# The next graph's input norm, moved from VectorE to ScalarE in two blocks of four tiles, in an attention loop with hand-written queues

## Chip, cores, metric

One core of one Trainium2 chip runs one program. The metric is the device time of one launch in microseconds (us). The kernel before takes 1538.24 us, the median of three runs (1538.18 to 1538.66).

## What is computed

Two layers over eight graphs of 1024 nodes with 128 features, all in fp32. The change lies in the second layer's graph attention, of which this is the reference, cut to what matters:

```
x = x + _L1_gnn_ref(_layernorm(x), adj, W_lin, b_lin, W_q, W_k, ln_g, ln_b)

X = heads(leaky_relu(xn @ W_lin + b_lin))           # 4 heads of 32 columns
q = heads(leaky_relu(xn @ W_q)); k = heads(leaky_relu(xn @ W_k))
att = sigmoid(einsum('bhxd,bhyd->bhxy', q, k) * scale)
adj_h = adj[:, None] * att
deg = sum(adj_h, -1); dis = where(deg > 0, deg ** -0.5, 0)
Y = (dis[..., :, None] * adj_h * dis[..., None, :]) @ X
out = layernorm(Y) * ln_g + ln_b
```

Here xn is `_layernorm(x)`, that is (x - mean) / sqrt(var + 1e-5) over the 128 features. Making xn of the next graph is the step that the change touches. Layer 1 (a graph convolution and a mixture of experts) and the layer after the attention (slices and a state-space mixer) are untouched.

## The kernel before

The program is a row of stages; `attention_gnn_stage` is the third and takes from about 668 to 1200 us of the profile. Each engine has a queue written out by hand: a double loop over i (B + 2 turns, i = 0 to 9) and n (16 steps), with semaphores between the engines. Nothing reorders a queue, so an instruction that waits holds up all behind it.

In turn i, step n stands for one of 2 x 8 pairs (half of the 1024 columns, tile of 128 rows) of graph i. Around it:

- TensorE: `products(i', n')` of 18 steps ago into YA, `scores(i, n)` into S (it waits for the sigmoid of the step before, since S has one buffer), `degrees` of two steps ago into DG (it waits for VectorE's multiply of that step), and a side job into the one buffer M. The list SIDE gives the side jobs by step: at 6 and 7 `x0` and `x1` (the product with W_lin), at 8 and 9 `xn0` and `xn1` (transposes of the next graph's normalised input X, which wait for `xn_ready`), at 3 and 5 `y0` and `y1`, at 2 and 10 the degrees, and the q and k products.
- ScalarE: the sigmoid of S into AH (128x2048, sets `att_ready`), and between sigmoids the copies out of PSUM.
- VectorE: `multiply(g)`, AH times the adjacency tile, 128x2048; between multiplies the small work: `stats_x(i + 1)` (statistics of the next graph's input, at step 4 for i = 0 and 1 and at step 0 for later i, by STATS_AT), `scale_X(i - 1, 1)` at step 4, `scale_Y` at 3 and 5, `stats_y` behind multiply(5), `make_X` ahead of multiply(6) and multiply(7), and so on. `apply_x(i + 1)` stands at step 6 for i = 0 and 1 and at step 4 for i = 2 to 6, behind multiply and, at step 4, behind `scale_X`. `apply_next`, for what follows the last graph, stands in turn 7.
- GpSimd: the power -0.5 of variances (`rstd_ready`) and of degrees, gathers of rows for graph i + 2 by indirect DMA, their sums (L1251, L1254), and the addition of a shift to R (L1287).
- SyncE: the loads of adjacency tiles and of X, and `keep_x`, which stores X before it is normalised in place (`x_kept`).

In the trace the input X bears the name `x`, YT the name `carry`. The norm's statistics and `apply` are in the class LayerNorm, lines 124 to 142: `apply` is eight VectorE instructions (x - mean) * rstd of 128x128 each, L142. Other lines of use: L1417 sigmoid, L1447 multiply, L1314 scores, L1327 products, L1341 degrees, L1370 the side product of x0 and x1, L1500 the tile product of scale_X, L1508 scale_Y, L1543 make_X. The front stage normalises on ScalarE with the same form as the change, at L777.

Of the kernel before, what the change touches and what calls it, by code (L numbers as in the profile page):

```python
# [7 lines left out]
ALU = mybir.AluOpType  # L8
ACT = mybir.ActivationFunctionType
AX = mybir.AxisListType  # L10

P = 128
B, N, D = 8, 1024, 128
T = N // P
# [16 lines left out]
STATS_AT = (4, 4)  # L31
# [11 lines left out]
class Chain:  # L43
# [13 lines left out]
    def wait(self):  # L57

        self.eng.wait_ge(self.sem, self.base + self.n)
# [1014 lines left out]
def is_graph(i):  # L1074
    return 0 <= i < B


def stats_step(i):

    return STATS_AT[i] if i < len(STATS_AT) else 0  # L1080
# [27 lines left out]
def attention_gnn_stage(nc, x_in, ys, slots, kept, X, W, Gt, xnT, Wc, YT, dis_last, x_out, adjT, b_lin, ln_g, ln_b, W_x, b_xT, W_sliceT, b_slice,  # L1108
# [6 lines left out]
    with ExitStack() as ctx:  # L1115
        sb = lambda name, shape, dt=fp32: ctx.enter_context(nc.sbuf_tensor("c_" + name, shape, dt))
        ps = lambda name, shape: ctx.enter_context(nc.psum_tensor("c_" + name, shape, fp32))
        sem = lambda name: ctx.enter_context(nc.semaphore("c_" + name))

        bias, gain, shift = sb("bias", [P, D]), sb("gain", [P, D]), sb("shift", [P, D])  # L1120
# [10 lines left out]
        DS = sb("DS", [P, HALF])  # L1131
        deg, mask, raw = sb("deg", [P, T, HEADS]), sb("mask", [P, T, HEADS]), sb("raw", [P, T, HEADS])
        dis = [sb("dis0", [P, T, HEADS]), dis_last]

        S = ps("S", [P, HEADS, HALF])
        YA = ps("YA", [P, NH, HALF])
# [6 lines left out]
        norm_in = LayerNorm(lambda n, s: sb("i" + n, s), lambda n: sem("i" + n))  # L1143
        norm_y = LayerNorm(lambda n, s: sb("y" + n, s), lambda n: sem("y" + n))
        pair_ready, x_ready, x_kept = sem("pair_ready"), sem("x_ready"), sem("x_kept")
        xn_ready = sem("xn_ready")
        side_full, side_free = sem("side_full"), sem("side_free")
        s_psum, att_ready = sem("s_psum"), sem("att_ready")
        ah_dve = sem("ah_dve")
# [238 lines left out]
        @block.scalar  # L1388
        def _(act):
            def copy_xnT(i, half):  # L1390
                act.wait_ge(side_full, full[f"xn{half}", i])
                act.activation(xnT[:, cols(half)], M[:, :], ACT.Copy).then_inc(side_free, 1)

            def copy_qk(dst, i, name):
                act.wait_ge(side_full, full[name, i])
                act.activation(dst[:, cols(int(name[-1]))], M[:, :], ACT.Copy).then_inc(side_free, 1)

            def copy_Y(i, half):
                wait(act, side_full, full[f"y{half}", i - 1] if i > 0 else 0)
                act.wait_ge(y_psum, STEPS * i + T * half + T)  # L1400
                act.activation(YT[:, cols(half)], YA[:, half, :], ACT.Copy).then_inc(yT_ready, 1)

            def copy_degrees(i, half):
                act.wait_ge(dg_psum, NH * i + half + 1)
                if half:
                    act.wait_ge(side_full, full["deg0", i])
                elif i > 0:
                    act.wait_ge(side_full, full["deg1", i - 1])
                act.activation(DS[:, :], DG[:, :], ACT.Copy).then_inc(ds_ready, 1)

            for i in range(B + 2):
                for n in range(STEPS):
                    g = STEPS * i + n
                    if is_graph(i):
                        act.wait_ge(s_psum, g + 1)
                        wait(act, y_psum, g - UNITS + 1)
                        act.activation(AH[g % UNITS][:, :, :], S[:, :, :], ACT.Sigmoid, scale=HD ** -0.5).then_inc(att_ready, 1)  # L1417
                    if n == 0 and is_graph(i):
                        copy_qk(K, i, "k1")
                    if n == 1 and is_graph(i):  # L1420
                        copy_qk(Q, i, "q1")
                    if n == 1 and is_graph(i - 1):
                        copy_degrees(i - 1, 1)
                    if n == 2 and is_graph(i - 2):
                        copy_Y(i - 2, 1)
                    if n == 9 and is_graph(i):
                        copy_degrees(i, 0)
                    if n == 10 and is_graph(i - 1):
                        copy_Y(i - 1, 0)
                    if i < B and n in (8, 9):  # L1430
                        copy_xnT(i + 1, n - 8)
                    if is_graph(i + 1):
                        if n == 11:
                            copy_qk(Q, i + 1, "q0")
                        if n == 13:
                            copy_qk(K, i + 1, "k0")

        @block.vector
        def _(dve):
# [39 lines left out]
                                            norm_in.rstd[(B - 1) % 2][:, t:t + 1], ALU.subtract, ALU.mult)  # L1479
                ins.then_inc(xn_ready, 1)  # L1480

            def apply_x(i):
                dve.wait_ge(x_kept, 16 * i)
                norm_in.apply(dve, X, X, i - 1, (i - 1) % 2).then_inc(xn_ready, 1)

            def read_degrees(i, half):
                dve.wait_ge(side_full, full[f"deg{half}", i])
# [60 lines left out]
            for i in range(B + 2):  # L1548
                for n in range(STEPS):
                    if n == 2 and is_graph(i - 1):  # L1550
                        read_degrees(i - 1, 1)
                    if n == 3 and is_graph(i - 2) and i - 2 < B - 1:
                        scale_Y(i - 2, 0)
                    if n == 5 and is_graph(i - 2) and i - 2 < B - 1:
                        scale_Y(i - 2, 1)
                    if n in (6, 7) and is_graph(i):
                        make_X(i, n - 6)
                    if n == 10 and is_graph(i):
                        read_degrees(i, 0)
                    if is_graph(i):  # L1560
                        multiply(STEPS * i + n)
                    if n == stats_step(i) and i < B:
                        stats_x(i + 1)
                    if n == 1 and is_graph(i):
                        leak_qk(K, i, "k1")
                    if n == 2 and is_graph(i):
                        leak_qk(Q, i, "q1")
                    if n == 4 and is_graph(i - 1):
                        scale_X(i - 1, 1)
                    if n == (6 if i < len(STATS_AT) else 4) and is_graph(i + 1):  # L1570
                        apply_x(i + 1)
                    if n == 4 and i + 1 == B:
                        apply_next()
                    if n == 7 and i + 1 == B:
                        fold_weights()
                    if n == 12 and i + 1 == B:
                        read_fold()
                    if n == 5 and is_graph(i - 2) and i - 2 < B - 1:
                        stats_y(i - 2)
                    if n == 8 and is_graph(i - 2) and i - 2 < B - 1:  # L1580
                        gain_Y(i - 2)
                    if n == 9 and is_graph(i - 2) and i - 2 < B - 1:
                        finish(i - 2)
                    if n == 12 and is_graph(i + 1):
                        leak_qk(Q, i + 1, "q0")
                    if n == 14 and is_graph(i + 1):
                        leak_qk(K, i + 1, "k0")
                    if n == 15 and is_graph(i):
                        scale_X(i, 0)
# [913 lines left out]
```

## Time and profile before

| | |
|---|---|
| median of three runs | 1538.24 us |
| the profiled execution | 1539.02 us |
| its span in the profile | 1537.3 us |
| TensorE busy | 91% of the span |
| VectorE busy | 66% |
| ScalarE busy | 49% |
| GpSimd busy | 47% |
| mean granted TensorE clock | 0.984 of full |

All times in the rows further down are in us from the start of the span, of this one profiled execution. A row of the view in order of time gives start, duration, engine, line, operation, output and inputs with their shapes, and how many instructions are merged in the row; the brackets give the idle time before it and what ended it. PE is TensorE, PEld its weight load, DVE VectorE, ACT ScalarE, POOL GpSimd. A merged row's duration runs from its first start to its last end.

### The profile page before, as it was taken

To read this page: it belongs to the slowest core of one execution; us is meant where nothing else is said; L and a number is where in the kernel's file an instruction comes from. 1 tells how busy PE (TensorE), PEld (TensorE's weight loads), DVE (VectorE), ACT (ScalarE), POOL (GpSimd) and SP (SyncE) were. 2 spreads that over 40 slices of the span, in tenths; PEclk is the share of its full clock that TensorE was granted. 3 is DMA by queue.
4 is the path that set the end of the run, shared out by engine and by line. 5 is a ranking of instruction groups with operands and counts; after the bars stand their busy time and mean duration, and the time that the engine had idled before them with its cause. 6 is when DMAs were issued, how large, how long until landed. Compare 5 with 4: busy or idle time off the path is not lost. (4 is left out here: it accounts for less than half of the span.)

```text
span 1537.3 us, 25067 instructions
## 1 busy us (share of the span) xinstructions
PE 1401.7 (91%) x9010; PEld 808.8 (53%) x9010; DVE 1021.2 (66%) x2212; ACT 748.2 (49%) x1184; POOL 720.7 (47%) x500
## 2 busy tenths in 40 slices
PE   4999999899999999977899988998999779999998
PEld 2455545669999998732222222222222357773488
DVE  2467767633333333368788999999987789967732
ACT  3365565534444444446454554655554457872110
POOL 1127776740000000749787887876233479981000
PEclk9999999999999999999999999999999999999999
DMA  9757637276788775633342424423322231004024
GB/s 300 254 188 282 235 118 228 88 205 203 229 230 231 233 228 159 171 118 125 96 129 90 124 84 122 142 84 119 91 90 69 69 95 42 15 1 90 1 85 138
DMA packets 207599, 215.26 MB, mean 140 GB/s; under 512 B 23269, under 2 KB 164709, under 8 KB 207476
## 3 DMA queue, kind: packets, MB, share of 16 engines
q1 hardware_dynamic: 199284, 196.81, 41.9%
q0 software_dynamic: 8192, 16.86, 3.5%
q8 instruction: 72, 1.18, 0.3%
q14 instruction: 51, 0.42, 0.1%
HBM read 168.54 MB, written 45.07 MB: 139 GB/s over the span
## 5 line engine op out<-in xcount | busy, mean ns | idle before, releaser
L1417 ACT ACTIVATE c_AH<-c_S 128x2048 f32<-128x2048 f32 x128 | 240.6, 1879 | 235.5 <-PE c_S L1314 235.5
L1447 DVE TENSOR_TENSOR c_AH<-c_AH,c_A 128x2048 f32<-128x2048 f32 x128 | 313.0, 2454 | 44.2 <-ACT c_AH L1417 43.9
L1242 POOL DMA_INDIRECT G<-ys,slots x102 | 195.4, 1915 | 32.7 <-issue 28.0
L810 ACT ACTIVATE a_A<-a_DG,a_A 128x256 f32<-128x256 f32 (+1 forms) x192 | 93.8, 527 | 208.3 <-PE a_DG L677 207.0
L530 POOL DMA_INDIRECT rows<-a_S,a_slots x128 | 134.0, 1047 | 49.9 <-issue 38.1
L557 POOL DMA_INDIRECT a_A<-ys,slots x16 | 16.4, 1024 | 292.9 <-DMA ys<-a_A 288.3
L1341 PE MATMUL c_DG<-c_AH,c_ones 128*32 128x512 f32 x1024 | 138.1, 612 | 12.0 <-DVE c_AH L1447 12.0
L1327 PE MATMUL c_YA<-c_AH,c_XT 128*32 128x512 f32 x1024 | 137.9, 620 | 12.1 <-DVE c_XT L1500 12.1
L1314 PE MATMUL c_S<-c_Q,c_K 32*128 32x512 f32 x928 | 135.2, 653 | 14.5 <-DVE c_K L1532 7.8
L648 PE MATMUL a_AG<-a_A,x 128*128 128x512 f32 x256 | 114.1, 599 | 5.1 <-DVE a_Z L891 5.1
L677 PE MATMUL a_DG<-a_A 128*128 128x256 f32 (+1 forms) x336 | 99.9, 420 | 7.1 <-ACT a_A L810 6.0
L690 PE MATMUL a_AG<-a_A 128*128 128x128 f32 x848 | 102.9, 277 | 0.0
L690 PEld LDWEIGHTS a_AG<-a_A 128*128 128x128 f32 x848 | 99.8, 194 | 3.5 <-issue 3.4
L1314 PEld LDWEIGHTS c_S<-c_Q,c_K 32*128 32x128 f32 x928 | 36.9, 186 | 116.6 <-ACT c_AH L1417 52.8
L690 PE MATMUL a_TP<-a_A 128*128 128x128 f32 x800 | 96.3, 275 | 0.0
L690 PEld LDWEIGHTS a_TP<-a_A 128*128 128x128 f32 x800 | 93.2, 192 | 2.9 <-issue 2.9
L1234 POOL TENSOR_TENSOR c_raw<-c_deg,c_power 128x16 f32<-128x16 f32 x16 | 73.0, 4562 | 36.0 <-DVE c_deg L1490 35.8
L677 PE MATMUL a_FG<-a_A 128*128 128x256 f32 (+1 forms) x312 | 86.0, 398 | 0.0
L648 PEld LDWEIGHTS a_AG<-a_A,x 128*128 128x128 f32 x256 | 47.3, 190 | 69.5 <-issue 59.4
L985 DVE COPY a_A<-a_AG 128x256 f32<-128x256 f32 x71 | 30.1, 424 | 75.0 <-PE a_AG L658 75.0
L1341 PEld LDWEIGHTS c_DG<-c_AH,c_ones 128*32 128x32 f32 x1024 | 20.4, 108 | 112.2 <-issue 83.8
L1697 POOL TENSOR_TENSOR s_SW<-s_SW,s_top 128x512 f32<-128x512 f32 x64 | 67.0, 1048 | 25.7 <-DVE s_top L1883 25.3
(393 smaller groups left out, 2566.2 us busy)
## 6 DMA issues: line engine op xcount, KB each, us to landing
a_A<-in_dram SPq DMA_DIRECT2D x72, 578.0 KB, 4.0
a_A<-in_dram SPq DMA_DIRECT2D x32, 1024.0 KB, 10.0
c_A<-in_dram SPq DMA_DIRECT2D x128, 256.0 KB, 2.8
a_A<-rows SPq DMA_DIRECT2D x71, 129.0 KB, 3.3
ys<-a_A SPq DMA_DIRECT2D x71, 128.0 KB, 2.3
a_X<-in_dram SPq DMA_DIRECT2D x8, 512.0 KB, 13.0
a_R<-in_dram SPq DMA_DIRECT2D x8, 512.0 KB, 5.3
stream<-a_R SPq DMA_DIRECT2D x8, 512.0 KB, 10.0
```

The lines of the kernel that those rows point to most:

```text
L530: pool.indirect_dma_start(rows, bass.IndirectOffsetOnAxis(ap=slots[:, k, T * i + t:T * i + t + 1], axis=0), S[i % 3][k][:, t, :], None, bo ...
L648: mm = pe.matmul(AG[:, half(h)], F[:, t, :], adj(i)[:, t, half(h)], start=(t == 0), stop=(t == T - 1))
L677: pe.matmul(up_bank(g, f)[:, 0:n], w_of(g)[:, f * P:(f + 1) * P], xT_of(g)[:, 0:n], start=True, stop=True).then_inc(up_psum, 1)
L690: mm = pe.matmul(YB[g % 2][:, t, :], hT[g % 2][:, f, t * P:(t + 1) * P], w_of(g)[:, F_N + FT + f * D:F_N + FT + (f + 1) * D], start=(f == ...
L810: act.activation(hT[g % 2][:, f, 0:size(g)], up_bank(g, f)[:, 0:size(g)], ACT.Gelu, bias=w_of(g)[:, F_N + f:F_N + f + 1]).then_inc(h_ready, 1)
L1234: pool.tensor_tensor(raw[:, tiles(half), :], deg[:, tiles(half), :], power[:, :].rearrange("p (t h) -> p t h", h=HEADS)[:, tiles(half), :] ...
L1242: pool.indirect_dma_start(Gt[k][:, t, :], None, ys, bass.IndirectOffsetOnAxis(ap=slots[:, k, T * i + t:T * i + t + 1], axis=0), bounds_che ...
L1314: mm = pe.matmul(S[:, h, :], keys[rows, t * P:(t + 1) * P], queries[rows, :], start=True, stop=True)
L1327: mm = pe.matmul(YA[h * HD:(h + 1) * HD, half, :], XT[:, t, h * HD:(h + 1) * HD], ah[:, h, :], start=(t == 0), stop=(t == T - 1))
L1341: mm = pe.matmul(DG[h * HD:(h + 1) * HD, :], ones[:, :], ah[:, h, :], start=(t == 0), stop=(t == T - 1))
L1417: act.activation(AH[g % UNITS][:, :, :], S[:, :, :], ACT.Sigmoid, scale=HD ** -0.5).then_inc(att_ready, 1)
L1447: dve.tensor_tensor(ah[:, :, :], ah[:, :, :], A[g % ADJ_BUFS][:, :].unsqueeze(1).to_broadcast([P, HEADS, HALF]), ALU.mult).then_inc(ah_dve, 1)
```

## The change

VectorE's eight instructions of `apply_x` become one, `make_offset`, which computes -mean * rstd for the eight tiles (128x8). ScalarE normalises with activations of the kind Identity, whose scale is rstd and whose bias is that offset, in place on X, in two blocks of four tiles. The first block stands behind the sigmoid of the step at which VectorE makes the offset, 6 in turns 0 and 1 and 4 in turns 2 to 6, the second behind the next step's sigmoid. `x_kept` is now waited for by ScalarE, and `xn_ready` is set by ScalarE's last tile.

```diff
+        offset = sb("offset", [P, T])
...
-        xn_ready = sem("xn_ready")
+        xn_ready, offset_ready = sem("xn_ready"), sem("offset_ready")
...
+            def apply_x(i, half):
+                u = (i - 1) % 2
+                act.wait_ge(offset_ready, i)
+                act.wait_ge(x_kept, 16 * i)
+                for t in range(4 * half, 4 * half + 4):
+                    ins = act.activation(X[:, t, :], X[:, t, :], ACT.Identity, bias=offset[:, t:t + 1],
+                                         scale=norm_in.rstd[u][:, t:t + 1])
+                if half:
+                    ins.then_inc(xn_ready, 1)
...
+                    at = n - (stats_step(i) + 2 if i < len(STATS_AT) else 4)
+                    if at in (0, 1) and is_graph(i + 1):
+                        apply_x(i + 1, at)
...
-            def apply_x(i):
-                dve.wait_ge(x_kept, 16 * i)
-                norm_in.apply(dve, X, X, i - 1, (i - 1) % 2).then_inc(xn_ready, 1)
+            def make_offset(i):
+                u = (i - 1) % 2
+                dve.wait_ge(norm_in.rstd_ready, i)
+                wait(dve, xn_ready, i - 1)
+                dve.scalar_tensor_tensor(out=offset[:, :], in0=norm_in.mean[u][:, :], scalar=-1.0, in1=norm_in.rstd[u][:, :],
+                                         op0=ALU.mult, op1=ALU.mult).then_inc(offset_ready, 1)
...
                     if n == (6 if i < len(STATS_AT) else 4) and is_graph(i + 1):
-                        apply_x(i + 1)
+                        make_offset(i + 1)
```

## Rows read from the trace of the kernel before

**Rows 1.** The page's first part, busy time and share of the span.
```profile
PE 1401.7 (91%) x9010; PEld 808.8 (53%) x9010; DVE 1021.2 (66%) x2212; ACT 748.2 (49%) x1184; POOL 720.7 (47%) x500
```
**Rows 2.** Windows view, attention stage: length; PE, PEld, DVE, ACT, POOL busy; clock; DMA.
```profile
668.00:1200.00 532.00, 476.06 (x3408) 132.22 (x3408) 474.18 (x660) 281.78 (x205) 359.39 (x155) 0.97 0.35 105
```
**Rows 3.** Line 777's view and row in time; ScalarE's groups in the slicing stage.
```profile
L777 ACT ACTIVATE a_xn<-a_X,a_shift,a_irstd x8: 478/478/493, 10.7 to 13.4; 128x128 f32<-128x128 f32 x8
...
10.72 3.18 ACT L777 ACTIVATE a_xn<-a_X,a_shift,a_irstd 128x128 f32<-128x128 f32 x8 [7.41 <-DVE a_shift L876]
...
L1827 ACT ACT_TABLE_LOAD x1 | 1.3, 1283 | 0.0
```
**Rows 4.** In order of time, turn 0, steps 7 to 10.
```profile
691.42 1.88 ACT L1417 ACTIVATE c_AH<-c_S 128x2048 f32<-128x2048 f32 x1 [1.28 <-PE c_S L1314]
...
695.53 1.14 PE L1314 MATMUL c_S<-c_Q,carry 32*128 32x512 f32 x8
...
696.84 2.15 DVE L142 TENSOR_SCALAR x<-x,c_imean,c_irstd 128x128 f32<-128x128 f32 x8
...
705.36 1.88 ACT L1417 ACTIVATE c_AH<-c_S 128x2048 f32<-128x2048 f32 x1 [0.50 <-PE c_S L1314]
```
**Rows 5.** In order of time, turn 1, steps 6 to 9.
```profile
748.48 1.93 PE L1327 MATMUL c_YA<-c_AH,c_XT 128*32 128x512 f32 x8 [6.01 <-DVE c_XT L1500]
...
757.52 1.88 ACT L1417 ACTIVATE c_AH<-c_S 128x2048 f32<-128x2048 f32 x1 [3.14 <-PE c_S L1314]
...
758.96 2.33 DVE L142 TENSOR_SCALAR x<-x,c_imean,c_irstd 128x128 f32<-128x128 f32 x8
...
760.46 1.14 PE L1314 MATMUL c_S<-c_Q,c_K 32*128 32x512 f32 x8
...
765.32 1.88 ACT L1417 ACTIVATE c_AH<-c_S 128x2048 f32<-128x2048 f32 x1 [1.28 <-PE c_S L1314]
```
**Rows 6.** In order of time, turn 3, steps 5 to 7; turns 2, 4, 5 alike.
```profile
877.24 1.88 ACT L1417 ACTIVATE c_AH<-c_S 128x2048 f32<-128x2048 f32 x1 [1.26 <-PE c_S L1314]
...
878.50 0.69 DVE L1500 TENSOR_TENSOR c_XT<-c_XR,c_dis 128x512 f32<-128x512 f32 x1
879.10 2.13 DVE L142 TENSOR_SCALAR x<-x,c_imean,c_irstd 128x128 f32<-128x128 f32 x8
...
879.57 1.02 POOL L1242 DMA_INDIRECT G<-ys,slots  x1 [0.30 <-issue]
...
880.24 1.14 PE L1314 MATMUL c_S<-c_Q,c_K 32*128 32x512 f32 x8
...
881.76 4.71 DVE L1447 TENSOR_TENSOR c_AH<-c_AH,c_A 128x2048 f32<-128x2048 f32 x1
881.95 2.36 POOL L1287 TENSOR_TENSOR c_R<-c_R,c_shift 128x1024 f32<-128x1024 f32 x1
...
889.53 1.16 PE L1370 MATMUL c_M<-W,xnT 128*128 128x128 f32 x8 [1.94 <-DVE c_XR L1543]
```
**Rows 7.** In order of time, sigmoid(8) of turns 2 and 5.
```profile
829.21 1.88 ACT L1417 ACTIVATE c_AH<-c_S 128x2048 f32<-128x2048 f32 x1 [8.07 <-PE c_S L1314]
...
1025.46 1.88 ACT L1417 ACTIVATE c_AH<-c_S 128x2048 f32<-128x2048 f32 x1 [5.36 <-PE c_S L1314]
```
**Rows 8.** In order of time, turn 6, steps 5 to 7.
```profile
1080.52 2.13 DVE L142 TENSOR_SCALAR x<-x,c_imean,c_irstd 128x128 f32<-128x128 f32 x8
...
1081.65 1.14 PE L1314 MATMUL c_S<-c_Q,c_K 32*128 32x512 f32 x8
...
1086.87 1.06 PE L1341 MATMUL c_DG<-c_AH,c_ones 128*32 128x512 f32 x8
...
1088.51 1.16 PE L1370 MATMUL c_M<-W,xnT 128*128 128x128 f32 x8 [0.57 <-DVE c_XR L1543]
```
**Rows 9.** In order of time, turn 1, steps 12 to 15.
```profile
780.72 2.50 POOL L1251 TENSOR_TENSOR G<-G 128x1024 f32<-128x1024 f32 x1
...
791.02 1.14 PE L1314 MATMUL c_S<-c_Q,c_K 32*128 32x512 f32 x8 [0.88 <-DVE c_K L1532]
```

## Prediction

> **What bounds the kernel now.** I read the busy shares first, then the windows of the attention stage, then its instructions in order of time, and last the rows that say what a waiting engine waited for. TensorE is busy for 91% of the span [rows 1]. The change lives in the attention stage alone, 532 us of the 1537.3 us span, where TensorE is busy 476 us, VectorE 474 us, ScalarE 282 us and GpSimd 359 us [rows 2]. Read as shares, VectorE (89%) is overfull and ScalarE (53%) half empty, so moving work from one to the other looks right. The reader should not stop there. Queues run in program order, and in this loop the next TensorE score product waits for the sigmoid just before it. ScalarE has free time, but none of it may be spent waiting at the wrong place.
>
> A graph's turn has 16 steps. In each, TensorE does scores(n), ScalarE sigmoid(n), VectorE multiply(n) (2.29 us alone). Between them stand the normalisations. Steps 5 to 8 are where a graph stalls: in the settled turns i = 2 to 5, ScalarE sits 8.07, 7.00, 6.71 and 5.36 us before sigmoid(8), waiting for scores(8) (four rows, of which the first and the last stand in [rows 7]). I follow who is last there, turn by turn, and redo the order of events with the new instructions.
>
> **What the change removes and adds.** For each of seven graphs VectorE loses eight subtract-and-multiply instructions, 2.13 to 2.33 us together [rows 4, 5, 6], and gains one on 128x8 numbers. Its nearest rows are the 0.16 to 0.18 us instructions of the norm's statistics; I take 0.17 us. ScalarE gains eight activations with bias and scale from a tile, in two blocks of four. The front stage has the same form: eight in 3.18 us, 0.478 us for one [rows 3]; so each further one costs (3.18 - 0.478) / 7 = 0.386 us and a block of four costs 0.478 + 3 x 0.386 = 1.64 us. In total ScalarE takes on 7 x 2 x 1.64 = 23 us, in a stage where it is free for 250 us. No DMA is added or moved.
>
> The new wait is what costs. Block 0 stands behind sigmoid(4) (i = 2 to 6) or sigmoid(6) (i = 0, 1) in ScalarE's queue and waits for the offset, which VectorE makes only after multiply of the same step, and that multiply needs this very sigmoid. Queued behind the waiting instruction is the next sigmoid, whose scores lie ready, and TensorE's next scores wait for that sigmoid. A sigmoid begins 0.1 us before the instruction ahead of it ends; TensorE starts 0.05 us after a sigmoid; scores to sigmoid is 1.21 us.
>
> **Turn i = 0, costs 2.8 us.** Now sigmoid(7) starts at 691.42, while VectorE's apply, thus the end of multiply(6), is at 696.84 [rows 4]. Afterwards: offset 696.84 to 697.01, block 0 697.05 to 698.69, sigmoid(7) 698.6 to 700.5, 7.2 us late. Scores(8), before at 695.53 [rows 4], start at 700.5; block 1 holds ScalarE to 702.0, so sigmoid(8) runs to 703.8; scores(9) 703.85; sigmoid(9) 705.1 to 706.9; sigmoid(10) 708.2. Before, sigmoid(10) began at 705.36 [rows 4]: most of the 7.2 us is taken back because VectorE's backlog held that stretch up anyway, 2.8 us are not. The following steps are 3.14 us each, the scores-sigmoid loop itself, so nothing later in this turn takes them back.
>
> **Turn i = 1, costs 2.2 us.** In times of before: apply began at 758.96 [rows 5]; block 0 to 760.84; sigmoid(7), before at 757.52, 760.74 to 762.62; scores(8), before at 760.46, 762.67; block 1 to 764.16; sigmoid(8) 764.06 to 765.94; scores(9) 766.3; sigmoid(9) 767.5 against 765.32 [rows 5].
>
> **Turns i = 2 to 5, cost nothing each.** The third graph shown: the tile product of scale_X ends at 879.19 and apply ran from 879.10 [rows 6]. The offset comes at 879.27, block 0 ends at 880.95, sigmoid(5) runs 880.85 to 882.73 instead of from 877.24, and scores(6) start at 882.8 instead of 880.24 [rows 6]: TensorE loses 2.5 us here. But in the second half of the stall VectorE is last, not TensorE. Multiply(5) takes 4.71 us there, twice its usual, because GpSimd's 128x1024 addition, begun at 881.95, takes 2.36 us of it [rows 6]. Afterwards multiply(5) could start at 882.8, finds GpSimd's addition running until 884.31, and needs 2.16 us more as it did before: it ends at 886.5 in both kernels. So do the statistics, make_X and the side product at 889.53, which TensorE now reaches after 1.94 us of waiting [rows 6]. From scores(6) to that side product TensorE needs, unhindered, (1086.87 - 1081.65) + 1.0 = 6.2 us (scores(6) and degrees(5) in [rows 8]); 882.8 + 6.2 = 889.0, still before 889.53. The 2.13 us taken off VectorE buy nothing, since its multiply waits for a later sigmoid and then for GpSimd; the sigmoid's 3.6 us cost nothing, since TensorE would have waited later. Bounds: -0.5 us each (TensorE's 889.0 if the lock goes the other way), +0.5 us if block 0 is slower than in the front stage; I take 0.1, two semaphore hops of 0.05.
>
> What hides the cost here is GpSimd's addition; where that cover is gone it shows. **Turn i = 6, costs 1.9 us.** There GpSimd added early, and multiply(5) is not stretched. Apply began at 1080.52 [rows 8]; block 0 to 1082.39; sigmoid(5) 1082.29 to 1084.17; scores(6) 1084.22 instead of 1081.65; the side product 6.2 us later, 1090.4, instead of 1088.51 [rows 8]. VectorE's make_X is ready at 1089.5, so TensorE is last.
>
> **What comes back.** In the second half of turn 1 GpSimd's queue of gathers and sums goes by its own time. Its sum at 780.72 stretches VectorE's work, and TensorE then waits 0.88 us for keys at 791.02 [rows 9] and 1.16 us for a multiply just before. If VectorE is 5 us later against it, that collision falls on steps with slack: 0 to 2.0 us back, I take 1.0 (nothing speaks for one end).
>
> **Sum.** 2.8 + 2.2 + 4 x 0.1 + 1.9 - 1.0 = 6.3 us. The profiled execution took 1539.02 us (span 1537.3), 0.8 above the median; it would take 1545.3, and the median 1538.24 becomes **1544.5 us**, +0.41%.
>
> One row speaks on whether VectorE's apply also held GpSimd up. A gather of GpSimd begun at 879.57, while apply ran, took 1.02 us, the shortest that any gather takes [rows 6]; so its removal sets GpSimd free of nothing, and the addition still starts at 881.95. The Trainium skill, page "GPSIMD Engine Reference", section "1. Specifications", says that GpSimd's SBUF interfaces are shared with VectorE's instructions in a two-port mode as well as with those of two SBUF inputs. By that rule apply, if it ran in such a mode, was in GpSimd's way, and the sum would be that of rival (d), 1542.5 us, instead of 1544.5. The trace agrees for the two-input multiply, and for apply it does not.
>
> **Rivals.** (a) *TensorE's clock, for the better.* The granted clock halves after some stalls: score and side products of the same form otherwise last 1.06 to 1.16 us then take some 2 (products(4) at 748.48 took 1.93, after 6.01 us of idleness [rows 5]). The stall before sigmoid(8) is 5.36 us where the clock stays full and 8.07, 7.00, 6.71 where not [rows 7]: 2.71 + 1.64 + 1.35 = 5.7 us over turns 2 to 4, and about 3 us more after TensorE's 6.0 us of idleness in turn 1. The change moves about 2.5 of TensorE's 3.4 idle microseconds of a turn some 5 us forward and parts them, so full speed may last. If all of these stretches vanish, 1544.5 - 8.7 and another 1.2 at the start of turn 6 give 1534.6, faster than before. It decides from over 9.4 us regained. If a part vanishes (3.2 to 9.4 us), the time is within 0.2% of before. For it: turn 5 shows the same idle times and no fall. Against: the sum of idleness stays. (b) *The clock, for the worse.* Turn 0 now has no fall, but will have 4.9 us of idleness in one piece (695.6 to 700.5), like the 6.0 us of turn 1; with a fall there (3 us) and full falls of 2.7 us in turns 2 to 6, 3 + 5 x 2.7 - 5.7 = 10.8 us more; half of that is 1550, all 1555. (c) *A table reload.* If the activation with bias were not in the sigmoid's table, each block would load twice, 28 loads; the slicing stage's one load row for exponentials, copies and the same biased form [rows 3] speaks against. Price 28 x 1.28 = 36 us, 1580. (d) *GpSimd's addition and multiply(5) part in turns 2 to 5.* Either the addition comes up to 2 us sooner because apply was in its way, or multiply(5) gets in before 881.95, for which sigmoid(5) would have to end 0.8 us sooner than worked out, with a block of 0.8 us instead of 1.64. Then TensorE's 889.0 is last: 4 x 0.5 us less, 1542.5. The gather of 1.02 us speaks against the one, the front stage's activations against the other.
>
> **Chances.** The forecast with small clock differences 0.62; (d) 0.05; (b) 0.10; (c) 0.02: slower by over 0.2% (about what a measurement of this kernel can tell from no change; above 1541.3) 0.79. Part of (a) within 0.2%: 0.15. All of (a), below 1535.2: 0.06. The range leaves out the far ends of (a), (b) and all of (c): 1539 to 1551 us.
>
> **What the profile of the changed kernel would show.** In turn 0, ScalarE idle 5 us or more between sigmoid(6) and block 0, ended by VectorE's offset, and sigmoid(7) 7 us late; in turns 2 to 5 the side product x1 released by VectorE's make_X as before, 11.0 us after the tile product of scale_X began, TensorE idle 2.5 us before scores(6), multiply(5) about 3.7 us long from 882.8; a block of four 1.64 us. The forecast is wrong if GpSimd's addition no longer meets multiply(5), if sigmoid(7) starts before the offset, or if the granted clock of the stage moves away from 0.97 [rows 2]: one hundredth of it is some 5 us.

## The result

| | median, us | runs | ratio to before |
|---|---|---|---|
| kernel before | 1538.21 | 1537.93 to 1538.66 | |
| the change | 1554.01 | 1548.31 to 1556.36 | 1.0097 (1.0069 to 1.0125) |
| the change, runs of `change_again` | 1555.65 | 1553.2 to 1558.0 | 1.0076 (1.0049 to 1.0103) |

The change makes the kernel 0.8 to 1.0% slower by the ratios; by the medians it is 15.8 and 14.2 us. 1544.5 was forecast, with a range up to 1551: the sign was right, the size was not, and the time lies outside the range. The profile below is of the fastest of its executions, 1548.31 us with a span of 1546.6, 9.3 us over the span of before; the median execution took 5.7 us more than this one. First the page's line of shares, against [rows 1], then the attention stage in the windows view, against [rows 2]:

```profile
PE 1410.7 (91%) x9010; PEld 814.4 (53%) x9010; DVE 998.5 (65%) x2163; ACT 769.2 (50%) x1240; POOL 722.6 (47%) x500
```
```profile
667.00:1210.00 543.00, 484.64 (x3420) 135.76 (x3420) 454.16 (x609) 303.09 (x261) 361.88 (x155) 0.95 0.34 103
```

The work moved as planned: VectorE has 23 us less, ScalarE 21 us more. TensorE has the same 9010 products and is busy 9 us longer, and the stage's granted clock fell from 0.97 to 0.95. That last figure is what the forecast lacked.

Turn 0 in order of time, against [rows 4]:

```profile
695.13 0.16 DVE L1500 SCALAR_TENSOR_TENSOR c_offset<-c_imean,c_irstd 128x8 f32<-128x8 f32 x1
...
695.33 1.65 ACT L1417 ACTIVATE x<-x,c_offset,c_irstd 128x128 f32<-128x128 f32 x4 [6.89 <-DVE c_offset L1500]
...
696.88 1.85 ACT L1428 ACTIVATE c_AH<-c_S 128x2048 f32<-128x2048 f32 x1
...
698.88 2.09 PE L1315 MATMUL c_S<-c_Q,carry 32*128 32x512 f32 x8 [4.99 <-ACT c_AH L1428]
...
700.90 1.94 PE L1342 MATMUL c_DG<-c_AH,c_ones 128*32 128x512 f32 x8
```

ScalarE stands 6.89 us in front of the offset with a sigmoid behind it whose scores are there; that sigmoid(7) comes 7.2 us late against the turn's start, and TensorE idles 4.99 us. Then the new thing: scores(8) take 2.09 us instead of 1.14 and the degrees behind them 1.94 instead of 1.07, which is the lower of the two granted levels, 1.2 instead of 2.4 GHz. I call it half clock below.

A settled turn, 3, against [rows 6] (times 4.75 us later than there up to sigmoid(4)):

```profile
884.05 1.65 ACT L1417 ACTIVATE x<-x,c_offset,c_irstd 128x128 f32<-128x128 f32 x4 [3.32 <-DVE c_offset L1500]
...
886.70 2.36 POOL L1288 TENSOR_TENSOR c_R<-c_R,c_shift 128x1024 f32<-128x1024 f32 x1
...
887.51 1.69 PE L1315 MATMUL c_S<-c_Q,c_K 32*128 32x512 f32 x8 [2.45 <-ACT c_AH L1428]
887.56 3.65 DVE L1461 TENSOR_TENSOR c_AH<-c_AH,c_A 128x2048 f32<-128x2048 f32 x1 [2.94 <-ACT c_AH L1428]
...
889.13 1.93 PE L1342 MATMUL c_DG<-c_AH,c_ones 128*32 128x512 f32 x8
...
895.32 1.16 PE L1371 MATMUL c_M<-W,xnT 128*128 128x128 f32 x8
896.41 1.06 PE L1328 MATMUL c_YA<-c_AH,c_XT 128*32 128x512 f32 x8
```

Up to multiply(5) all went as worked out: 2.45 us of idleness before scores(6), multiply(5) 3.65 us long because GpSimd's addition holds it until 889.06. But scores(6) and what follows run at half clock for a while, and TensorE reaches the side product x1 at 895.32, 1.0 us later in the turn than before, with no wait: TensorE was last there, not VectorE's make_X. Behind x1 the products then keep full clock, where the kernel before had half clock in this place:

```profile
890.62 1.91 PE L1327 MATMUL c_YA<-c_AH,c_XT 128*32 128x512 f32 x8
```

So sigmoid(8) of turn 3 comes 0.6 us sooner in its turn than before: the half clock moved from behind x1 to in front of it, and the two nearly cancel.

Turn 6, against [rows 8]:

```profile
1077.43 3.31 POOL L1288 TENSOR_TENSOR c_R<-c_R,c_shift 128x1024 f32<-128x1024 f32 x1
...
1079.71 3.18 DVE L1461 TENSOR_TENSOR c_AH<-c_AH,c_A 128x2048 f32<-128x2048 f32 x1 [1.19 <-ACT c_AH L1428]
...
1087.27 2.09 PE L1315 MATMUL c_S<-c_Q,c_K 32*128 32x512 f32 x8 [2.45 <-ACT c_AH L1428]
...
1089.29 1.94 PE L1342 MATMUL c_DG<-c_AH,c_ones 128*32 128x512 f32 x8
...
1091.16 1.92 PE L1371 MATMUL c_M<-W,xnT 128*128 128x128 f32 x8
```

Two things the sum did not have: three groups of products in a row at half clock (0.95 + 0.88 + 0.76 us over their usual 1.14, 1.06 and 1.16), and GpSimd's addition, which in the kernel before began 2.6 us ahead of sigmoid(4) and here 0.3 us ahead, so that multiply(4) takes 3.18 us instead of 2.29.

### The profile page after: what moved, and what is told of

Read it like the earlier page. It is cut to its first block and busy times, and to the rows that moved or that the text cites. A ratio compares the mean times of both kernels' runs of the same rounds, so it can differ in the third digit from the quotient of the medians.

```text
span 1546.6 us, 25087 instructions
## 1 busy us (share of the span) xinstructions
PE 1410.7 (91%) x9010; PEld 814.4 (53%) x9010; DVE 998.5 (65%) x2163; ACT 769.2 (50%) x1240; POOL 722.6 (47%) x500
## 5 line engine op out<-in xcount | busy, mean ns | idle before, releaser
L1461 DVE TENSOR_TENSOR c_AH<-c_AH,c_A 128x2048 f32<-128x2048 f32 x128 | 308.3, 2416 | 72.1 <-ACT c_AH L1428 71.6
L1243 POOL DMA_INDIRECT G<-ys,slots x102 | 201.5, 1975 | 36.3 <-issue 27.9
L1315 PE MATMUL c_S<-c_Q,c_K 32*128 32x512 f32 x928 | 138.4, 667 | 25.1 <-ACT c_AH L1428 18.0
L557 POOL DMA_INDIRECT a_A<-ys,slots x16 | 16.4, 1024 | 294.6 <-DMA ys<-a_A 290.1
L1342 PE MATMUL c_DG<-c_AH,c_ones 128*32 128x512 f32 x1024 | 142.7, 630 | 7.7 <-DVE c_AH L1461 7.7
L1235 POOL TENSOR_TENSOR c_raw<-c_deg,c_power 128x16 f32<-128x16 f32 x16 | 69.8, 4364 | 38.3 <-DVE c_deg L1507 38.1
```

The costliest lines, as they stand in the source:

```text
L1235: pool.tensor_tensor(raw[:, tiles(half), :], deg[:, tiles(half), :], power[:, :].rearrange("p (t h) -> p t h", h=HEADS)[:, tiles(half), :] ...
L1243: pool.indirect_dma_start(Gt[k][:, t, :], None, ys, bass.IndirectOffsetOnAxis(ap=slots[:, k, T * i + t:T * i + t + 1], axis=0), bounds_che ...
L1315: mm = pe.matmul(S[:, h, :], keys[rows, t * P:(t + 1) * P], queries[rows, :], start=True, stop=True)
L1342: mm = pe.matmul(DG[h * HD:(h + 1) * HD, :], ones[:, :], ah[:, h, :], start=(t == 0), stop=(t == T - 1))
L1461: dve.tensor_tensor(ah[:, :, :], ah[:, :, :], A[g % ADJ_BUFS][:, :].unsqueeze(1).to_broadcast([P, HEADS, HALF]), ALU.mult).then_inc(ah_dve, 1)
```

## The account by turns

The start of each sigmoid says how far the attention loop has come. The table gives, for stretches of the stage, how many us more a profiled execution needed than the one of before. It is worked out from the starts of the sigmoids; the last line counts what products at half clock took over their usual length, summed over the stage, in us (13.3 in the profile of before; how merged rows are counted moves each of these sums by about 1 us).

| stretch | forecast | change | change_again | change_gathers_filler |
|---|---|---|---|---|
| turn 0 | 2.8 | 4.5 | 5.0 | 2.8 |
| turn 1, steps 6 to 9 | 2.2 | 2.9 | 3.1 | 2.4 |
| turn 1, end | -1.0 | -1.6 | -1.6 | 0.0 |
| turns 2 to 5 | 0.4 | -0.4 | 2.8 | 1.3 |
| turn 6, start | 0 | -1.4 | -1.4 | -1.4 |
| turn 6, steps 4 to 15 | 1.9 | 5.2 | 5.5 | 2.7 |
| turn 7 | 0 | 3.0 | 3.0 | 1.4 |
| sum | 6.3 | 12.1 | 16.4 | 9.2 |
| half clock, over the usual | as before | 20.7 | 22.3 | 9.1 |

With the stretches ahead of sigmoid(1) and behind sigmoid(127) (-1.7 and -1.1; -0.3 and +0.1) the second and third columns give the whole spans, 9.3 and 16.2 us more. One thing stands in every column: the profile of before itself has a hold-up at the start of turn 6, where GpSimd's sums come late (explained below). Profiles without it get 2.4 us back at sigmoid(0) of turn 6, which the line of turns 2 to 5 contains, and 1.4 us by sigmoid(1), which is the line "turn 6, start". From sigmoid(0) to sigmoid(15) of each, turns 2 to 5 of the change cost -0.5, -0.6, 1.0 and 0.8 us, 0.7 together. The experiments explain the last column and why the others differ.

## The experiments

The runs came in four lots, and the chips differ: the second and third lot ran where the kernel before takes 1541.5 and 1539.6 us, the first and the fourth where it takes 1572.8 and 1574.1 us and single executions spread over 17 to 19 us (15.5 where it takes 1541.5). There the timing decides little, and I read the profiles. The change itself was not timed on the chip of the first lot.

### One part of the change alone

Only turns 0 and 1 on ScalarE:

```diff
-                    if at in (0, 1) and is_graph(i + 1):
+                    if at in (0, 1) and is_graph(i + 1) and i < 2:
...
-                        make_offset(i + 1)
+                        (make_offset if i < 2 else apply_whole)(i + 1)
```

> ScalarE applies only in turns 0 and 1; in turns 2 to 6 VectorE applies as before. Worked-out cost of the wait: 2.8 + 2.2 us, less 0 to 2 us that come back in turn 1, so 1541 to 1544. If half clock of TensorE in the longer idle stretches is the larger part of the change's cost (the profile of the change shows sigmoid(10) of turn 0 4.5 us late instead of 2.8), 1543 to 1547. If the cost lies in ScalarE's added work as such, 2/7 of 15.8 us: 1542.7, with turns 0 and 1 not special.

Measured 1571.97 us, ratio 1.0001 (0.9964 to 1.0037). The interval holds the forecast's 5 us as well as no change. By the profile turns 0 and 1 cost 4.2 and 2.7 us, 6.9 together, nearly as in the change, and half clock follows the idle stretch in both; nothing comes back at the end of turn 1 (0.0 us, against 1.6 in the change); turns 2 to 4 cost 0.2 us together. In turn 6 the loop still lost 0.9 us, with the addition again 0.3 us ahead of sigmoid(4): this goes with where GpSimd's addition falls, not with a wait in turn 6 (before_gathers, with nothing on ScalarE and the addition at the same place, loses the same 0.9 us there).

The counterpart (`i >= 2` in both places, offsets counted from graph 3):

> ScalarE applies only in turns 2 to 6; turns 0 and 1 as before. Worked-out cost of the wait: 4 x 0.1 + 1.9 us: 1540.5. If the clock is the larger part: turn 6 alone was 5.3 us late in the profile of the change and turns 2 to 5 differ from execution to execution, 1544 to 1550, with a spread of several us between executions. If it is ScalarE's added work as such, 5/7 of 15.8 us: 1549.5.

Measured 1570.68 us, ratio 1.0009 (0.9985 to 1.0033). In the profile the delay is -1.0 us before turn 2, -2.1 at the start of turn 4, -1.1 at that of turn 5 and -0.3 at the end of turn 5, then -2.7 at the start of turn 6, where the kernel before has its late sum. So turns 2 to 5 cost 0.7 us, turn 6 costs 5.2 us, turn 7 3.0. The two parts have their cost where the waits show, and the settled turns have nearly none, as forecast. "ScalarE's added work as such" would have cost 2.2 us in every one of these five turns, 0.7% together; the interval leaves that out, and the profile shows no such even cost.

### The wait without the work

```diff
                 act.wait_ge(x_kept, 16 * i)
-                for t in range(4 * half, 4 * half + 4):
-                    ins = act.activation(X[:, t, :], X[:, t, :], ACT.Identity, bias=offset[:, t:t + 1],
-                                         scale=norm_in.rstd[u][:, t:t + 1])
-                if half:
-                    ins.then_inc(xn_ready, 1)
...
                         make_offset(i + 1)
+                        apply_whole(i + 1)
```

> VectorE makes the offset and then applies itself as before; ScalarE waits for the offset at the change's two places and does no tile. If the wait is the cost: sigmoid(7) of turn 0 at 697.1 instead of 691.4, and block 0's 1.64 us is missing from each delay, so turn 0 about 1.2 us, turn 1 about 0.6 us, turn 6 about 0.3 us and with VectorE's apply still there some 2 us more in turns 2 to 6 where multiply(5) waits for both: 1540 to 1546. If ScalarE's tiles cost, the time is that of before, 1538.5.

Measured 1576.18 us, ratio 1.0024 (1.0000 to 1.0047). In the profile (of an execution 8 us above the median) sigmoid(7) of turn 0 is 5.6 us late, exactly the wait; turn 0 costs 3.2 us and turn 6 2.8, more than the 1.2 and 0.3 expected, with half clock in both. Turn 1 costs -0.1 us where 0.6 was expected and the change has 2.9. So in turns 0 and 6 6.0 of the change's 9.7 us are there without a single tile on ScalarE; the cost of turn 1 does not show without the tiles.

### The blocks one step later

```diff
-                    at = n - (stats_step(i) + 2 if i < len(STATS_AT) else 4)
-                    if at in (0, 1) and is_graph(i + 1):
+                    at = n - (5)
+                    if at in (0, 1) and is_graph(i + 1) and i >= 2:
```

> As t26_only, but each block of four stands one step later, behind sigmoid(5) and sigmoid(6): then the offset is there 0.2 us after sigmoid(5), nothing is queued behind a long wait, and multiply(5) can start 2 us before GpSimd's addition. If the wait behind the sigmoid is what costs, and VectorE's relief then counts: TensorE's waits of 0.99 and 1.94 us in turns 2 to 5 go, 3 us each and some half clock with them, so 1522 to 1532, faster than the kernel before. If ScalarE's added work as such costs, it is as slow as t26_only.

Turns 0 and 1 are VectorE's here, as in t26_only, so that run is the one to compare with. Measured 1566.31 us, ratio 0.9969 (0.9942 to 0.9997) beside t26_only's 1.0009: with the same work on ScalarE, but behind sigmoids whose wait is over, it is 4.4 us under t26_only by the medians and just clear of the kernel before. It is not the 1522 to 1532 us that I had expected. The profile is of the slowest of its seven executions (1581.59 us), and its attention stage takes 8.1 us more than in the profile of before. It shows both the gain at steps 5 to 8, 3.6 us in turn 3, and where it goes; here the start of turn 4:

```profile
952.56 4.45 POOL L1252 TENSOR_TENSOR G<-G 128x1024 f32<-128x1024 f32 x1
957.09 4.27 POOL L1255 TENSOR_TENSOR x<-x,G 128x1024 f32<-128x1024 f32 x1
...
959.09 2.82 DVE L1553 SCALAR_TENSOR_TENSOR c_K<-c_K 128x512 f32<-128x512 f32 x1
...
961.96 2.09 PE L1315 MATMUL c_S<-c_Q,c_K 32*128 32x512 f32 x8 [4.26 <-DVE c_K L1553]
```

GpSimd sums the gathered rows, VectorE's work on the keys takes 2.82 us instead of 0.69 beside it, and TensorE waits 4.26 us, and then runs at half clock. From sigmoid(8) of turn 3 to sigmoid(1) of turn 4, 5.1 us go back. In this profile GpSimd's queue has become what decides the turn. Over all profiles its first sum begins at one of few distances from sigmoid(11): 4.5 to 4.9 us, 7.0 to 8.5, or 11.2 to 12.5; and the next turn's first sigmoid follows sigmoid(15) after 3.5 to 3.9, 5.1, or 7.4 to 8.2 us. The kernel before has a late one (7.5 us) in one turn of five, the change in its first profile in none, late_blocks in its profile in all five.

### More executions of the change, and a filler for TensorE

> The change itself, unaltered, for more executions and a second profile beside runs of the kernel before on the same chip. By the worked-out waits alone 0.4% slower than the kernel before; if half clock comes on top, 0.7 to 1.2% slower, and the times of single executions fall where the mean granted clock rises, about half a us per us at half clock. In the profile, products at about twice their length stand behind the idle stretch before scores(6) in turns 2 to 6 and before scores(8) in turns 0 and 1.

Measured 1555.65 us beside 1541.46. The account by turns is above. Against the first profile it has one late sum of GpSimd (11.4 us, then 8.2 us) at the end of turn 3, and turns 2 to 5 need 3.2 us more. So what a turn costs depends on which of the three distances it falls into and on whether the clock falls; the two profiles differ by that, and I take it that the other executions do. In turn 3 of this profile the clock did not fall behind the 2.45 us of idleness, and there everything goes as forecast: TensorE reaches x1 0.5 us ahead and make_X releases it.

```profile
888.39 1.14 PE L1315 MATMUL c_S<-c_Q,c_K 32*128 32x512 f32 x8 [2.45 <-ACT c_AH L1428]
...
895.15 1.16 PE L1371 MATMUL c_M<-W,xnT 128*128 128x128 f32 x8 [0.48 <-DVE c_XR L1560]
```

```diff
+                again = 1
+                if what == "x1":
+                    again = {0: 4, 1: 3}.get(i, 1)
+                if what == "y1" and i <= 4:
+                    again = 4
...
-                    for c in range(4):
+                    for c in [c for _ in range(again) for c in range(4)]:
```

> The change, and TensorE repeats side products in the time in which it would idle: y1 of turns 2 to 6 four times instead of once (+1.8 us of work), x1 of turn 0 four times, of turn 1 three times (+3, +2 us). Same results, no other edit. If the clock makes up the part of the cost that the worked-out waits don't, fewer half-clock stretches in turns 0 to 6 and 4 to 9 us faster than change_again. If the waits alone are the cost, the same time as change_again or 1 to 3 us slower.

Measured 1554.33 us, ratio 1.0066 (1.0040 to 1.0092); 1.3 us under change_again, which can't be told from nothing. The granted clock did rise (0.975 to 0.980 by the executions' medians). Turn 0 shows the effect cleanly:

```profile
696.81 1.65 ACT L1422 ACTIVATE x<-x,c_offset,c_irstd 128x128 f32<-128x128 f32 x4 [6.89 <-DVE c_offset L1505]
...
700.36 1.14 PE L1315 MATMUL c_S<-c_Q,carry 32*128 32x512 f32 x8 [2.31 <-ACT c_AH L1433]
701.43 1.07 PE L1342 MATMUL c_DG<-c_AH,c_ones 128*32 128x512 f32 x8
```

ScalarE waits the same 6.89 us, TensorE idles 2.31 us instead of 4.99, its products keep their 1.14 and 1.07 us, and turn 0 costs 2.8 us, the forecast to the tenth. But two turns had GpSimd's sums late (8.2 and 7.7 us to the next sigmoid), and in turn 6 scores(6) and degrees(5) fell to half clock in spite of the repeats (4.4 us there), so the whole did not get shorter by what the clock gave. To separate the two I had to set GpSimd's queue right first.

### GpSimd's queue

Two levers: the addition of the shift done by VectorE, and three gathers moved ahead of a wait.

```diff
-                    pool.tensor_tensor(R[:, :, :], R[:, :, :], wide(shift), ALU.add).then_inc(shifted, 1)
...
+            def shift_R(i):
+                dve.wait_ge(r_loaded, 16 * (i + 1))
+                dve.tensor_tensor(R[:, :, :], R[:, :, :], shift[:, :].unsqueeze(1).to_broadcast([P, T, D]),
+                                  ALU.add).then_inc(shifted, 1)
...
                         gain_Y(i - 2)
+                        shift_R(i - 2)
```
```diff
-                gather(i + 2, range(4, 8))
+                gather(i + 2, range(4, 11))
...
-                gather(i + 2, range(8, 16))
+                gather(i + 2, range(11, 16))
```

> The kernel before, with the addition of the shift to R moved to VectorE in the same way. GpSimd's addition then no longer stretches multiply(5), which decides steps 5 to 8 there: it takes 2.29 us instead of 4.7, the side product x1 comes about 2.3 us sooner in turns 2 to 5, 0.6% faster than before if nothing gives it back. If the addition was not what VectorE was late by, no change.

Measured 1542.74 us beside 1541.46, ratio 1.0006 (0.9986 to 1.0026). Steps 5 to 8 gained (turn 3: 4.1 us), and 6.1 us went back from there to sigmoid(1) of the next turn: all four settled turns now have the late sum, 12.5 us and 8.2 us.

> late_blocks, and the addition of the shift to R is done by VectorE behind gain_Y (1.2 us in a stretch with slack) instead of by GpSimd (2.4 us). late_blocks gained 3.6 us per turn at steps 5 to 8 in its profile and gave up to 3.7 us back at the start of the next turn, where GpSimd's sums stretch VectorE's work on the keys. If GpSimd's queue is what gives it back, taking 2.4 us off it per turn brings 1.5 to 3 us of each turn: 1.0 to 1.5% faster than the kernel before. If not, as late_blocks, 0.3% faster.

Measured 1536.05 us, ratio 0.9955 (0.9934 to 0.9975), half of what was hoped for; its sums are still late in turns 2 to 5 (11.4 us). Taking work off GpSimd was not enough, since its queue still stood waiting for VectorE's statistics of Y.

> late_blocks_shift_on_vector, and three of the eight gathers that GpSimd does behind the power for norm_y now stand ahead of it, in the time (5.3 us in that profile) in which GpSimd waits for VectorE's statistics. If GpSimd's queue decides the turn there (its first sum begins 11.4 us after sigmoid(11) began, and the next turn's first sigmoid comes after 7.4 to 8.2 us instead of 5.1 or 3.8), the sum comes some 4 us sooner, the interval is 5.1 or less, and turns 2 to 5 are 3 us shorter each: 1.2 to 1.6% faster than the kernel before. If GpSimd isn't what decides, 0.45% faster as late_blocks_shift_on_vector.

Measured 1518.37 us beside 1539.63, ratio 0.9864 (0.9845 to 0.9882), 21 us faster than the kernel before and the fastest of all. Turn 3, against the 11.4 us of late_blocks (sigmoid(11) began at 895.73):

```profile
903.94 2.62 POOL L1252 TENSOR_TENSOR G<-G 128x1024 f32<-128x1024 f32 x1
906.64 2.71 POOL L1255 TENSOR_TENSOR x<-x,G 128x1024 f32<-128x1024 f32 x1
```

8.2 us, and 5.1 us to the next turn's first sigmoid, in every turn; half clock over the usual is 6.4 us in the stage instead of 13.3.

> late_blocks (shift still added by GpSimd) with the same three gathers moved ahead. If GpSimd's queue took back what the later blocks gained (11.4 us and 8.2 us in all its turns), 0.9 to 1.4% faster than the kernel before. If not, 0.3%.

Measured 1523.75 us, ratio 0.9898 (0.9875 to 0.9920): without the moved addition 15.9 of the 21.3 us remain.

> The kernel before with the three gathers moved ahead. Its sums begin 7.1 us after sigmoid(11) in most turns and the interval is 5.1 us; one turn in five is late (11.4 and 7.5 us). If the queue's phase matters: the intervals become 3.8 us, 0.2 to 0.4% faster. If not: no change.

Measured 1532.47 us, ratio 0.9952 (0.9934 to 0.9970). So the gathers alone bring 7.2 us, and ScalarE's blocks in turns 2 to 6, one step later than in the change, bring 8.7 us on top (late_gathers). The gain of before_gathers is at steps 5 to 8 as well, because GpSimd's addition now comes behind the gathers, 13.5 us after sigmoid(4) instead of 7.8, and no longer meets multiply(5). Turn 3:

```profile
878.77 2.29 DVE L1447 TENSOR_TENSOR c_AH<-c_AH,c_A 128x2048 f32<-128x2048 f32 x1
...
884.12 1.16 PE L1370 MATMUL c_M<-W,xnT 128*128 128x128 f32 x8 [0.58 <-DVE c_XR L1543]
```

> The change with the three gathers moved ahead; ScalarE's wait is left as it is. Turns 0, 1 and 6 keep their delays of 4.5 to 5.0, 3 and 5.3 us (waits plus half clock), so at least 0.5% slower than before_gathers. If late sums of GpSimd are a part of what the change costs (3.3 us in one turn of change_again, none in the change's first profile), it is 0.2 to 0.4% faster than change_again; if not, the same time.

Measured 1550.46 us, ratio 1.0073 (1.0056 to 1.0089). This pair is the test of the cover named in the forecast. With the addition out of the way the kernel before gains 4.1 us by sigmoid(8) in turn 3, of which 2.5 go back by sigmoid(9), and the change nothing (it loses 0.6):

```profile
884.68 1.65 ACT L1417 ACTIVATE x<-x,c_offset,c_irstd 128x128 f32<-128x128 f32 x4 [3.32 <-DVE c_offset L1500]
...
888.19 2.29 DVE L1461 TENSOR_TENSOR c_AH<-c_AH,c_A 128x2048 f32<-128x2048 f32 x1 [2.94 <-ACT c_AH L1428]
...
890.16 1.94 PE L1342 MATMUL c_DG<-c_AH,c_ones 128*32 128x512 f32 x8
...
897.15 1.16 PE L1371 MATMUL c_M<-W,xnT 128*128 128x128 f32 x8
```

Multiply(5) has its 2.29 us, but it starts 2.9 us idle behind the delayed sigmoid, and TensorE is last on the way to x1. Where the cover is gone, the wait and the half clock behind it cost in every turn: 1.2 to 1.8 us in each of turns 2 to 5, 6.1 together. The two kernels differ by 18 us, where change and before differ by 14 to 16.

### The clock, with the sums on time

> change_gathers once more, on the same chip as change_gathers_filler, as what that is compared with: 0.7% slower than the kernel before.

Measured 1582.67 us, ratio 1.0068 (1.0043 to 1.0094).

> change_gathers with the repeated side products of change_filler. In change_filler the half-clock time fell (7 us less of it in TensorE's work), but GpSimd's sums were late in two turns, and the time hardly moved. With the gathers ahead the sums aren't late. If the half clock is the part of the change's cost that the worked-out waits lack: 4 to 8 us faster than change_gathers_again. If it isn't: the same or slower by what the filler adds.

Measured 1575.23 us, ratio 1.0028 (0.9991 to 1.0064): by the ratios 0.4% or 6 us less than its neighbour, by the medians 7.4. The executions spread over 22 us here and the two intervals overlap, so I lean on the profiles: turn by turn it lies 1.2, 0.2, 2.9 and 1.6 us under change_gathers_again in turns 0, 1, 6 and 7, 4.9 us over the stage. Turn 6:

```profile
1118.40 3.19 DVE L1466 TENSOR_TENSOR c_AH<-c_AH,c_A 128x2048 f32<-128x2048 f32 x1 [1.19 <-ACT c_AH L1433]
...
1125.98 1.14 PE L1315 MATMUL c_S<-c_Q,c_K 32*128 32x512 f32 x8 [2.46 <-ACT c_AH L1433]
1127.05 1.07 PE L1342 MATMUL c_DG<-c_AH,c_ones 128*32 128x512 f32 x8
1128.05 1.16 PE L1376 MATMUL c_M<-W,xnT 128*128 128x128 f32 x8
...
1132.20 1.16 PE L1376 MATMUL c_M<-W,xnT 128*128 128x128 f32 x8
```

The same 2.46 us of idleness as in the change stand before scores(6), and all products keep their full-clock lengths. TensorE was busy with repeated transposes up to shortly before; that alone is not enough, since the same 16 transposes and the same 2.45 us of idleness in turn 6 of change_filler were followed by half clock. From scores(6) to x1 it is 6.22 us, the 6.2 of the forecast. What is left in turn 6, 2.7 us, is the 1.9 of the wait and the 0.9 of the longer multiply(4).

## Why the prediction was right and wrong

- *A block of four costs 1.64 us.* Right: 1.65 and 1.64. *No table reload.* Right: ScalarE's instructions rose by 56 activations, 1184 to 1240, and by nothing else.
- *Block 0 waits for VectorE, with a ready sigmoid behind it; turn 0.* Right in all steps: sigmoid(7) 7.2 us late as worked out. The cost of 2.8 us holds where the clock stays full (2.8 in both filler profiles); in the change it was 4.5 and 5.0. The term was mis-sized by 1.7 and 2.2 us, the half clock behind the 4.99 us of idleness, which I had found (rival b) and left out of the sum.
- *Turn 1, 2.2 us.* 2.9 and 3.1; 2.4 in change_gathers_filler, where the products behind the wait keep full clock: the same.
- *Turns 2 to 5 cost nothing, since GpSimd's addition makes VectorE last.* Right for the cover: the pair before_gathers and change_gathers showed it by taking it away, and turn 3 of change_again went as worked out. The size, 0.7 us from step to step in the first profile and 0.7 in t26_only, is in part luck: in the other settled turns the half clock uses up the 0.5 us by which TensorE was ahead at x1 and makes TensorE last, so the sign named for these turns (x1 released by make_X) did not come there; and the same turns no longer have the half clock that turns 2 to 4 of before had behind x1. I also did not see that GpSimd's sums at the end of these turns have their own timetable.
- *Turn 6, 1.9 us.* 5.2 and 5.5. The wait is right in size (2.7 with full clock, less 0.9); missing were 2.6 to 2.8 us of half clock and the 0.9 us because GpSimd's addition moved against multiply(4).
- *Turn 7, nothing.* 3.0 us. Work there is unchanged, but TensorE, idle 1.20 us at step 11 in both kernels, falls to half clock behind it in the change and not before (3.2 us of products over their length in both profiles). It fell in late_shift_gathers and also in before_gathers and before_shift_on_vector, which have nothing on ScalarE, and not in t01_only, wait_alone or change_filler. What decides it is open; the filler makes no repeats in that turn.
- *1.0 us comes back at the end of turn 1.* 1.6 in both profiles of the change, where GpSimd's sums kept their time and the loop fell behind them (the first sum 4.5 us after sigmoid(11) instead of 8.1). But nothing came back in t01_only, which has the same turns 0 and 1, in change_gathers or in the filler profiles: there the sum begins 7.0 to 8.1 us after sigmoid(11), so it had moved with the loop. The forecast's premise that this queue goes by its own time holds in some profiles only, so that the number came is partly luck.
- *Rivals.* (a) was wrong in sign, (c) and (d) did not come. (b) is what happened: it had 10.8 us as its full price and a chance of 0.10.
- *The step that failed.* The sum has no term for TensorE's clock: turns 0, 6 and 7 were worked out with every product at its full-clock length. The only reason given stands against rival (a), "the sum of idleness stays". That sum did stay, 135.6 us of the span before and 135.9 in the change, and the half clock rose all the same, from 13.3 to 20.7 and 22.3 us: what counted was where the idleness fell. Turn 0 measured 4.5 and 5.0 instead of 2.8, turn 6 5.2 and 5.5 instead of 1.9 (0.9 of it GpSimd's addition), turn 7 3.0 instead of nothing. The forecast's own sign for this came true, the stage's granted clock left 0.97 for 0.95. The rows of before already spoke for a term: the long waits of turns 1 to 4 (6.01 us; 1.94 us behind 0.99) and the 4.28 us at the start of turn 6 were followed by half clock, only turn 5 with the same 1.94 us was not; and the change put 4.99 and 2.45 us of idleness ahead of scores(8) of turn 0 and scores(6) of turn 6, where there had been none.

The Trainium skill, page "TensorE: Matmul & The Clock Gate", Part 1, says that the array's clock is halved when the engine has not been busy enough of late and given back after sustained work. The trace agrees: products of 1.14 us took 2.09 behind 4.99 us of idleness, and the same products 1.14 behind 2.31 us where repeated side products stood ahead of the wait; without repeats, in wait_alone, they took 2.09 behind 2.33 us.

Of the change's 14 to 16 us, then, some 7 to 8 us are the waits themselves with the 0.9 us of turn 6 (2.8, 2.4 and 2.7 us in turns 0, 1 and 6 of change_gathers_filler; change_filler shows the same only for turn 0). Most of the rest is half clock, 7 to 9 us more of it than before in the two profiles of the change, part of it hidden. A late sum of GpSimd adds about 4 us where it comes (4.4 in change_again, 3.8 in the profile of the kernel before, which has one too). Taking half clock away brought 7.4 us by the medians of change_gathers_filler and change_gathers_again and 4.9 by their profiles, but their intervals overlap; the shares of the last two differ between executions, and the timing does not fix them.

## What to carry to other kernels

A half-idle engine in a hand-written queue has time but not at every place: before moving work to it, look at what is queued behind the new instruction and what the instruction waits for. In turns 2 to 6 the same activations cost behind the sigmoid that feeds their own producer (t26_only, turn 6: 5.2 us) and gained 8.7 us when they stood one step later and GpSimd's gathers were out of the way. When a wait moves to TensorE, let one end of the range have the products behind it at half clock; here gaps of one length were followed by either level. And after every gain in one stretch ask which engine has its own timetable: here in the profile of late_blocks 5 to 6 us per turn went back where GpSimd's sums came late, until three of its gathers were moved into a wait of its own. Blocks one step later, gathers and addition moved together brought the largest gain, 1.4%.

## What the runs showed of the hardware

- GpSimd's 128x1024 additions and VectorE's 128x2048 products did not run side by side: whichever began second ended about its own length after the other's end (multiply 4.71 us instead of 2.29 with an addition of 2.36 inside; in turn 6 of the change the addition 3.31 us instead of 2.36 and multiply(4) 3.18 instead of 2.29).
- The length of one idle stretch did not decide TensorE's level. Behind the 2.45 us before scores(6) half clock came in all five of turns 2 to 6 in the first profile of the change, but not in turn 3 of change_again nor in turn 5 of change_gathers; behind 1.94 us it came in turns 2 to 4 of the kernel before and not in turn 5; with repeats ahead of it, it came in turn 6 of change_filler (2.45 us) and not in that of change_gathers_filler (2.46 us). What decides it is open. A fall behind one of these cost 1.4 to 2.7 us of longer products.
- The profiles from different chips differ ahead of the attention stage. From 300 to 400 us of the span, the kernel before on the first chip and t01_only (the same code there) on another; columns as in [rows 2], the last is GB/s moved by DMA:

```profile
300.00:400.00 100.00, 97.16 (x626) 81.39 (x625) 38.64 (x103) 40.54 (x84) 22.37 (x22) 1.00 0.67 198
```
```profile
300.00:400.00 100.00, 87.10 (x517) 68.91 (x517) 33.48 (x92) 32.07 (x64) 21.71 (x22) 0.91 0.49 148
```

  148 GB/s instead of 198, with TensorE busy 87.1 us instead of 97.2; wait_alone and late_blocks, on t01_only's chip, moved 121 and 124 in that stretch. The attention stage begins 26.5 us later in t01_only than in the profile of before and 36 to 39 us later in those two, which is most of the difference in span. What holds the transfers up I did not follow. Within the attention stage the sigmoids of the two chips agree to 0.01 us over whole turns.
